# Decoder block on one core: choosing the experts before an eviction, and the rank products before the next transposes

## The reference, cut to what matters

```
x = x + causal_linear_attention(layernorm(x))      # 16 heads of 16
x = x + cross_attention(layernorm(x), ctx_1024)    # 77 keys per batch
x = x + ffn(layernorm(x), index_b, index_t)
```

```
shared_out    = ln(silu(x @ sw1.T + sb1) * (x @ sw2.T + sb2)) @ sw3.T + sb3
x_moe         = x[index_b, index_t]
expert_scores = sigmoid(x_moe @ eg_w.T + eg_b)
top1_idx      = argmax(expert_scores + exp_bias)
weights       = softmax([sigmoid(x_moe @ sg_w.T + sg_b), expert_scores[top1_idx]])
out[index]    = shared_out[index] * weights[0] + expert_out[top1_idx] * weights[1]
```

## Time and profile before

| what | value |
|---|---|
| median of 3 runs | 381.33 us (381.18 to 382.5) |
| span of the profiled execution, first to last instruction | 377.9 us |
| time of the profiled execution by itself | not listed; the span is 3.4 us under the median |
| TensorE / VectorE / GpSimd / ScalarE busy | 356.6 / 296.1 / 279.1 / 162.6 us |
| mean granted clock of TensorE | 0.988 of full speed |

### The profile page before, as it was taken

One profiled execution on the slowest core, in us unless ns is written; L12 is line 12 of the kernel. 1 busy time (PEld: TensorE's weight loads), 2 busy tenths in 40 slices (PEclk: granted clock), 3 DMA queues, 4 the chain that ended last, 5 costly groups with the idle time before them and its releaser, 6 DMA issues. The chain is left out here.

```text
span 377.9 us, 10670 instructions
## 1 busy us (share of the span) xinstructions
PE 356.6 (94%) x3514; PEld 255.6 (68%) x3514; DVE 296.1 (78%) x922; ACT 162.6 (43%) x394; POOL 279.1 (74%) x414
## 2 busy tenths in 40 slices
PE   8999999999999999999999999999899989998781
PEld 4566677777677777767777777778676556655451
DVE  2588788898989898888898878886756588799462
ACT  2463553454455346436436524442456435331120
POOL 5338987766777866877867789898978888578455
PEclk9999999999999999999999999999999999999897
DMA  8993881200300120032121013003000233148750
GB/s 255 328 308 88 251 245 22 66 16 16 72 31 16 35 53 16 19 83 87 55 49 39 25 25 67 16 20 80 16 31 28 73 97 111 57 146 283 220 181 23
DMA packets 39309, 34.50 MB, mean 91 GB/s; under 512 B 4505, under 2 KB 38456, under 8 KB 39256
## 3 DMA queue, kind: packets, MB, share of 16 engines
q1 hardware_dynamic: 36392, 29.54, 27.7%
q0 software_dynamic: 1312, 3.37, 2.9%
q10 hardware_dynamic: 1552, 0.92, 0.9%
HBM read 17.55 MB, written 12.60 MB: 80 GB/s over the span
## 5 line engine op out<-in xcount | busy, mean ns | idle before, releaser
L1650 POOL TENSOR_TENSOR s_t<-s_t,causal 128x512 f32<-128x512 f32 x63 | 78.9, 1273 | 15.6 <-ACT s_t L961 15.4
L539 PE MATMUL bank<-h1t,w_qkv 128*128 128x512 f32 x112 | 52.9, 595 | 0.4 <-DVE x L1220 0.3
L1207 DVE TENSOR_TENSOR s_t<-sbank,causal 128x512 f32<-128x512 f32 x65 | 43.5, 671 | 1.1 <-PE sbank L560 1.0
L1642 POOL TENSOR_TENSOR state_wide<-state,own_pair 128x256 f32<-128x256 f32 x28 | 18.9, 676 | 25.5 <-DVE state L1198 24.4
L961 ACT ACTIVATE s_t<-sbank 128x512 f32<-128x512 f32 x63 | 33.7, 587 | 7.8 <-PE sbank L560 7.8
L560 PE MATMUL sbank<-arena 32*128 32x256 f32 x512 | 36.7, 400 | 0.0
L599 PE MATMUL bank<-s_t,vp 128*32 128x128 f32 x1024 | 34.6, 275 | 1.1 <-DVE s_t L1207 0.4
L546 PE MATMUL bank<-w_qkv,h1t 128*128 128x256 f32 x128 | 34.2, 389 | 0.0
L1658 POOL TENSOR_TENSOR rr<-ve,neg_half 128x3 f32<-128x3 f32 x36 | 31.9, 887 | 3.0
L684 PE MATMUL bank<-w_out,attn_t 128*128 128x256 f32 x128 | 33.6, 385 | 0.5 <-DVE attn_t L1288 0.5
L778 PE MATMUL sbank<-h1t,w 128*128 128x512 f32 x72 | 33.0, 596 | 0.5 <-ACT h1t L961 0.5
(11 more groups left out here) (231 smaller groups left out, 831.5 us busy)
## 6 DMA issues: line engine op xcount, KB each, us to landing
rden_t<-rden SPq DMA_DIRECT2D x64, 64.0 KB
rows<-x SPq DMA_DIRECT2D x32, 128.0 KB, 1.7
x<-in_x SPq DMA_DIRECT2D x7, 512.0 KB, 8.6
out<-x SPq DMA_DIRECT2D x7, 512.0 KB
we<-in_we SPq DMA_DIRECT2D x1, 2048.0 KB
xmask<-in_mask POOLq DMA_DIRECT2D x2, 616.0 KB, 10.3
rows<-empty SPq DMA_DIRECT2D x1, 1032.0 KB, 5.2
we<-in_we SPq DMA_DIRECT2D x1, 1024.0 KB
```

Of the source, the lines that this page charges most:

```text
L539: mm = pe.matmul(dst[:, :], w_qkv[:, ch, cb * P:(cb + 1) * P], h1t[:, g % 3, ch, :], start=(ch == 0), stop=(ch == CH - 1))
L1207: dve.tensor_tensor(s_t[:, r, :, :], sbank[r][:, :].rearrange("p (s q) -> p s q", s=4), causal[:, :].unsqueeze(1).to_broadcast([P, 4, P]), ...
L1650: pool.tensor_tensor(s_t[:, r, :, :], s_t[:, r, :, :], causal[:, :].unsqueeze(1).to_broadcast([P, 4, P]), ALU.mult)\
```

## The change

In round 6 VectorE adds the gate bias and chooses the experts first, and evicts unit 4 behind that. TensorE makes the rank products first, and transposes unit 7 behind them. No instruction is added or removed.

```diff
@@ TensorE, round q @@
+                if q == GATHERED:
+                    route_ranks(pe)
                 if q != FIRST_M - 1:
                     to_features(pe, q + 1)
-                if q == GATHERED:
-                    route_ranks(pe)
                 y_products(pe, q - 1, expert, load_expert if q == FIRST_M - 1 else None)
@@ VectorE, round q @@
                 if q == FIRST_M + 1:
                     normalize_blocks(q - 1)
-                y_evict(q - 2, 0, 2 if FIRST_M + 2 <= q <= NU else GT)
                 if q == GATHERED:
                     add_gate_bias()
                     choose_experts()
+                y_evict(q - 2, 0, 2 if FIRST_M + 2 <= q <= NU else GT)
                 if q != FIRST_M + 1:
                     normalize_blocks(q - 1)
```

## The result

The changed kernel takes 382.55 us (median of 22 runs, 381.17 to 383.88), the kernel before 380.76 on the same chips (22 runs, 379.48 to 382.95). The ratio is **1.0048**, 95% interval 1.0033 to 1.0063: 1.8 us slower (380.76 x 0.0048), with bounds of 1.3 and 2.4. The interval leaves out 1, so the change is slower. The forecast was +1.50, within the 0.5% that the prediction takes as no difference; the measured ratio is within it too, its upper bound is not.

What follows compares the result with a forecast made beforehand. The chain from VectorE's slots, not TensorE, was taken to set the end. With L1464 held, L1360 starts at 329.19 instead of 327.69: 381.33 + 1.50 = 382.83, say 382.8, range 380.7 to 383.9.

Steps and rivals of the forecast that it cites:

- The slots set the end: Chain from VectorE's slots through indirect stores, loads and M units: what moves the slots moves the end by as much.
- The hold at L1464: VectorE's choice: L1464 held until GpSimd's bias of group 5 ends, L1360 starting 1.50 later; chance 0.47.
- Each mark named in advance: Profile after: L1452 near 322.6, L1360 near 329.2, first indirect store at 334.0, L882 near 327.8.
- A: VectorE's choice: only instructions with two inputs are held, L1466 first; +0.88, 382.2; chance 0.18.
- B: VectorE's choice: small instructions slip through, nothing held beside GpSimd's bias; -0.57, 380.8; chance 0.14.
- Rival C: VectorE held twice, L1360 also waiting for GpSimd's L1692; one gives +2.1, both +2.8; chance 0.13.
- Its condition: GpSimd's L1692 comes first if TensorE's transposes end more than a moment before VectorE's evictions; worked-out times differ by 0.01.
- its price: Each free L1692 on GpSimd takes 0.76 or less, so each costs L1360 up to 0.63.
- Rival D, the clock: TensorE in 355 to 360, granted 0.66: avoiding that gives 381.1, another such stretch 384.5; chance 0.08, half each way.
- TensorE and the queues: `y_products(5)` about 1.0 later, hidden by VectorE's delay of 1.50; store 4 some 4.5 later on SyncE's queue, costing nothing.
- The sum: Whole kernel: +1.50 added to the median 381.33, forecast 382.8.

Runs made afterwards that it cites:

- vector_part: Kernel before with only VectorE's new order, TensorE's order as before; ratio 1.0038 (1.0009 to 1.0067).
- tensor_part: Kernel before with only TensorE's new order; ratio 0.9973 (0.9950 to 0.9996), measured again 0.9989 (0.9966 to 1.0013).
- log_in_psum: Changed kernel with ScalarE's exponential written to PSUM, so L1464 reads PSUM; one run, time not read, L1439 to first indirect store 11.80.
- no_bias5: Changed kernel without GpSimd's bias of group 5, a small memset keeping the signal; ratio 0.9975 (0.9944 to 1.0007).
- bias_early: Changed kernel with group 5's bias ahead of unit 4's inverse root on GpSimd, fourth bias part moved; ratio 0.9991, again 0.9979.
- old_order_late_bias: Kernel before with GpSimd's bias of group 5 held back until L1452 is done, so beside the choice; ratio 1.0065 (1.0042 to 1.0088).
- half_bias: Changed kernel with group 5's bias added to two of its four tiles only; one run, time not read, L1464 took 1.07.
- bias_early_old_order: Kernel before, old order on VectorE and TensorE, group 5's bias ahead of unit 4's inverse root, fourth bias part moved; ratio 1.0042.

## Why the prediction was right

**What bounds the stretch.** The slots set the end, as said: the chain that ended last goes through the slots and the indirect stores of L1816, before and after. In `vector_part` and `tensor_part` it goes on through SyncE's queue and the weights instead of ScalarE's wait, but still from the last of these stores. Runs with a reach of +1.51, +2.22 and +1.45 came out at 1.0048 (and 1.0038 for the same reach), 1.0065 and 1.0042, those with -0.39 to -0.54 at 0.9972 to 0.9991. The times alone could not rank the faster ones: `tensor_part`, with the reach of before, lies among them at 0.9973 and 0.9989, so that the gains of the faster kernels rest on the reach, and the loss of the slower ones on both.

**The hold at L1464.** The step decided the sign: without it the sum was -0.57. It was taken from one cast, which was no small instruction, and from the rule cited beside it; it held for 36 elements to within 0.01 (+1.51 against +1.50). Each mark named in advance was there once the 0.65 is taken off: the choice started at 323.30 - 0.65 = 322.65 for 322.6, L1360 at 329.20 for 329.19, the first indirect store at 334.04 for 334.0, L882 at 327.76 for 327.8.

**Rivals A and B** were not alternatives but other kernels: A is what `log_in_psum` does (+0.90 for +0.88), B what `no_bias5` and `bias_early` do (-0.48 and -0.54 for -0.57). B is 0.09 short in `no_bias5`, where L1452 started 1.04 after L1439 for the 0.97 that were worked out, and 0.03 in `bias_early`, where the choice and the evictions took 0.03 more than their sum.

**Rival C** did not come: L1360 started at 329.85, GpSimd's first L1692 at 329.97, and GpSimd lost the tie as before (1.53 for two). Two steps of it were off. Its condition was met and did not decide: the transposes ended at 328.64 + 1.06 = 329.70, 0.24 before the evictions (329.94), as the ranks passed in 0.23 (328.41 to 328.64) and not 0.49, but L1692 starts 0.27 after the transposes. And its price was too high: two free L1692 take 1.10 (`vector_part`), 0.55 each and not 0.76, so a hold by one costs some 0.4 and not 0.63. But the second hold it feared is real: `old_order_late_bias` shows one of 0.21 by that very instruction.

**Rival D, the clock,** was underrated as a nuisance. It moved the way from L1816 to the last store of the output by 1.1 between the two profiled executions, in favour of the changed kernel. It tells nothing of the change.

**TensorE and the queues.** `y_products(5)` started 1.11 later (330.08 - 0.65 against 328.32) for 1.0. It was hidden as said: it ended at 330.08 + 1.96 = 332.04, and VectorE came to evict it only at 335.62. `vector_part` is no test of this, since its product comes as late (329.28 - 321.49 = 7.79 against 7.80 from L1439).

**The size.** The sum was +1.50 and the times give 1.8 with 1.3 to 2.4 as bounds. The reach accounts for 1.51; the 0.3 between is within the interval and has no cause shown. That the time itself, 382.55, came so near to the 382.8 forecast is in part luck: the kernel before was 0.57 faster in this series (380.76) than the 381.33 that the forecast started from.

## What to carry to other kernels

Before work is moved into an idle stretch of VectorE, look at what GpSimd does in it, and at where the operands of the moved instructions lie: an eviction from PSUM with one SBUF tensor passed beside GpSimd's work at full speed, a 36-element instruction from SBUF to SBUF stood for 2.0 us. In a chain of small steps that each wait for the one before, a hold at one step delays all that follow by its full length, so such a chain should get the stretch free of GpSimd's long instructions, and the evictions the other one. Where the end scatters by more than the effect, measure the distance between two instructions that enclose the change.

## What the runs showed of the hardware

The hold has a sharp end. In the kernel before (three places), `half_bias` and `old_order_late_bias`, a held instruction ended as if it had begun 0.13 to 0.15 before GpSimd's instruction ended, whatever its own length (0.17 to 0.68) and however long it had waited (0.07 to 2.0). The cast of `bias_early_old_order` (0.14) fits as well. The other way round it is the same: the third indirect store of the kernel before ended as if it had begun 0.13 before VectorE's L1360 ended. L1464 of the changed kernel fits: 325.97 - 0.18 = 325.79, 0.15 before 325.94.

Not every instruction from SBUF to SBUF is held. The reciprocal with one source of 128x36 took its 0.38 in the middle of the bias, where the tensor_scalar of the same size stood still. The Trainium skill, SBUF — State Buffer, Who interferes with whom, names copy, cast and tensor_scalar in their two-port modes, and any two SBUF inputs against a GpSimd instruction that reads SBUF, as what contends for the port pair shared with GpSimd. These runs agree for cast and tensor_scalar, and for two inputs beside the bias and the normalization, not for two inputs beside the inverse root (L1466 of `bias_early`). The reciprocal, which it does not name, was free.

What ScalarE waits for ahead of its first L1088 in the M units stays open. The wait of 5.95 in the chain is 5.87 in the changed kernel and 6.47 in `bias_early`, always with an unnamed releaser and beside the weight loads. In `vector_part` and `tensor_part` the chain that ended last went through these loads instead. No run was aimed at it.
